# Router products and co-attention weights moved into the normalization of a twelve-layer decoder kernel

## The chip, the cores and the metric

One core of one Trainium2 chip runs the whole program. The metric is the device time of one launch in microseconds (us), as the median of several executions. TensorE is called PE below, VectorE DVE, ScalarE ACT, GpSimd POOL, and SyncE (which issues all DMAs here) SP.

## The reference, cut to what matters

A decoder with four levels works on `x` of 4 batches x 512 tokens x 128 features. Each of its twelve sublayers computes `x = x + f(layernorm(x))`. Three of them are mixtures of experts (stages `l0m`, `l1m`, `l3m` of the kernel, with 16, 64 and 32 experts), and one is a co-attention with a context of 77 tokens per batch (`l1c`). What the change touches of them:

```python
# every expert sublayer, h = layernorm(x)
scores = sigmoid(h @ router_w.T)              # (tokens, experts)
# top groups and top experts of scores + bias; weights w from the chosen scores
out = sum over chosen experts of w * (silu(h @ gate) * (h @ up)) @ down  + shared expert(h)

# co-attention, h = layernorm(x), c = context
similarity = h . w1 + c . w2 + (h * w3) . c + b   # (tokens, 77), softmax over both sides follows
out = [parts made of c, h and the two softmaxes] @ W_qv + b_qv
x = x + out
```

## The kernel before

The program is a row of stages. Each stage is a function that opens blocks (`nc.Block()`); in a block every engine has its own instruction list, and no engine goes on to the next block before all engines have finished this one. Semaphores order the work inside a block. Nothing is scheduled by a planner: each engine runs what the function lists for it, in that order.

Every stage begins with `layernorm` (line 100), one block: DVE and ACT normalize 16 token tiles of `T.X` into `T.LNX` (L142, L171), PE transposes them batch by batch into four PSUM banks (L162), and the banks are copied into `T.LNT`, batches 0 and 2 by ACT (L176) and batches 1 and 3 by DVE (L149). `T.LNT` holds features on partitions and tokens along the row.

`expert_ffn` (line 882) is the expert stage. In the block behind the normalization PE first makes the router products of all 16 tiles (L1079), then the shared expert (`shared_up`, L1028 and L1029, and `shared_down`, L1035). A float32 product of 512 columns shows as two matmul instructions. Meanwhile ACT rounds `T.LNT` into `x_hi` (L1155) and the first expert weights into `w_hi` (L1121), and POOL makes the remainders `x_lo` (L1207) and `w_lo` (L1203). When the router products are there, ACT takes the sigmoid (L1160, `score`), and DVE selects the groups and experts (`route`: L1305, L1280 to L1291, L863 to L868, L1316 to L1335, L1356), with products of the shared expert (L1236) put between its steps. The combine weights are then transposed (L1100), copied, stored and fetched again by SP, and the expert loop begins. PE may run two shared products ahead of DVE (`AHEAD = 2`). In stage `l3m` the weights come as bfloat16 and ACT first widens router and shared weights (L1150, L1153).

`l1_coattention` (line 1582) makes two small arrays first on DVE: `c3`, the context times w3 plus w1 (L1719), and `w2` (L1720). PE then makes the product L1685, after it the similarities of a batch (L1624), and DVE and ACT the softmax over the context (`centre`, `exponentials`, `normalize`: L1732 to L1743). POOL adds the bias to all of `T.X` (L1793), which `close(0)` waits for. Names in the trace drop trailing digits, so `l1c_c` is `c3` and `l1c_w` is `w2`, `w14` or the weights.

## Time and profile before

| | |
|---|---|
| median of 3 runs | 2343.5 us (2336.73 to 2348.67) |
| the profiled execution, its own time | 2343.47 us |
| its span in the trace | 2341.7 us |
| busy: PE, DVE, ACT, POOL | 2088.5, 1676.8, 1215.5, 1153.7 us |
| where the four stages begin (their normalization's first DMA) | l0m 322.4, l1c 484.7, l1m 546.5, l3m 2190.6 us |

The time is what the host's clock on the device gives for a launch; the span is from the first to the last recorded instruction. Busy time of an engine says nothing about which engine is waited for at a given place; that has to be read at that place.

### The profile page before, as it was taken

How to read it: one execution, taken by the hardware profiler on the slowest of the kernel's cores; microseconds unless marked ns; L12 is line 12 of the kernel's file. 1: busy time of each engine (PE TensorE's matmuls, PEld its weight loads, DVE VectorE, ACT ScalarE, POOL GpSimd, SP SyncE). 2: the span in 40 equal slices, each digit the busy share in tenths (PEclk: the TensorE clock that was granted, in tenths of full speed). 3: DMA queues.
4: the chain of work that ended last, by engine and by line, in shares of the span. 5: the costliest groups of instructions: out<-in, count | busy, mean ns of one | idle time of the engine just before them, and what ended most of it. 6: DMA issues, size and time to landing. Idle time of an engine off the chain costs nothing. (4 is left out here: it accounts for less than half of the span.)

```text
span 2341.7 us, 37726 instructions
## 1 busy us (share of the span) xinstructions
PE 2088.5 (89%) x12788; PEld 1458.2 (62%) x12788; DVE 1676.8 (72%) x3556; ACT 1215.5 (52%) x2598; POOL 1153.7 (49%) x1344
## 2 busy tenths in 40 slices
PE   6999779768999987759999999999999986879888
PEld 3666557555788865536666666666666644547666
DVE  5777767756788875557777777777766664469578
ACT  6888645523566653625445444544444443444455
POOL 5333026201699960148776666667666613004255
PEclk8999979968999999979999999999999998989899
DMA  1000007000776620023333433333343331000085
GB/s 51 3 3 3 8 18 160 8 6 22 170 156 155 156 68 1 14 72 60 90 95 84 106 72 100 87 98 95 84 92 72 80 92 42 1 1 1 14 205 124
DMA packets 65048, 161.92 MB, mean 69 GB/s; under 512 B 8139, under 2 KB 19147, under 8 KB 57560
## 3 DMA queue, kind: packets, MB, share of 16 engines
q1 hardware_dynamic: 64856, 159.50, 29.1%
q8 instruction: 103, 1.69, 0.3%
q14 instruction: 89, 0.73, 0.1%
HBM read 156.46 MB, written 3.01 MB: 68 GB/s over the span
## 5 line engine op out<-in xcount | busy, mean ns | idle before, releaser
L2821 ACT ACTIVATE l2h_prT<-bank 128x512 f32<-128x512 f32 x256 | 151.8, 593 | 261.9 <-PE bank L2708 261.9
L2719 PE MATMUL bank<-l2h_og,l2h_wo 128*128 128x512 f32 x512 | 260.3, 592 | 1.6 <-DVE LNT L2980 1.6
L2829 ACT ACTIVATE l2h_pr<-twin,l2h_nmx 128x512 f32<-128x512 f32 x256 | 175.8, 687 | 155.7 <-PE bank L2708 127.8
L1215 POOL TENSOR_TENSOR l1m_hid_lo<-l1m_hid,l1m_hid_hi 128x512 fp32r<-128x512 f32 x128 | 209.8, 1658 | 45.8 <-ACT l1m_hid_hi L1142 45.3
L2956 DVE TENSOR_TENSOR l2h_vg<-bank,l2h_gv 128x512 f32<-128x512 f32 x256 | 175.4, 685 | 76.6 <-PE bank L2682 62.1
L3058 POOL TENSOR_TENSOR l2h_vs<-l2h_vg 128x256 f32<-128x256 f32 x256 | 188.7, 737 | 32.0 <-DVE l2h_vg L2956 31.8
L2983 DVE TENSOR_REDUCE l2h_nmx<-twin 128x2 f32<-128x1024 f32 x128 | 156.1, 1220 | 46.9 <-PE twin L2697 46.8
L3053 POOL TENSOR_TENSOR l2h_plain<-l2h_plain,l2h_rotated 128x512 f32<-128x512 f32 x64 | 82.1, 1283 | 211.2 <-DVE l2h_rotated L2949 211.2
L2968 DVE TENSOR_TENSOR l2h_og<-bank,l2h_gt 128x512 f32<-128x512 f32 x256 | 173.2, 679 | 2.2 <-PE bank L2719 1.6
L2708 PE MATMUL bank<-ident,l2h_pr 128*128 128x128 f32 x1024 | 161.4, 280 | 0.6 <-ACT l2h_prT L2821 0.6
L2708 PEld LDWEIGHTS bank<-ident,l2h_pr 128*128 128x128 f32 x1024 | 117.3, 141 | 69.4 <-issue 46.4
L2682 PE MATMUL bank<-l2h_w_hi,l2h_x_hi 128*128 128x512 f32 x256 | 149.8, 585 | 4.4 <-DVE l2h_vg L2956 4.3
L405 ACT ACTIVATE l0a_pr<-l0a_sc,l0a_nmx 128x128 f32<-128x128 f32 (+3 forms) x256 | 133.3, 553 | 22.1 <-DVE l0a_nmx L290 21.2
L1265 DVE TENSOR_TENSOR l1m_hid<-l1m_prod,l1m_c 128x512 f32<-128x512 f32 x128 | 136.5, 1066 | 4.4
L3061 POOL TENSOR_TENSOR l2h_vs<-l2h_vs 128x128 f32<-128x128 f32 x256 | 122.4, 478 | 20.1
L2733 PE MATMUL bank<-l2h_prT,l2h_v 128*64 128x256 f32 x1024 | 124.6, 385 | 0.0
L1177 ACT ACTIVATE l1m_gate<-bank 128x512 f32<-128x512 f32 x128 | 76.6, 599 | 85.5 <-PE bank L1020 85.5
L2439 POOL TENSOR_TENSOR l3x_pr<-l3x_pr,l3x_rs 128x1232 f32<-128x1232 f32 x16 | 36.0, 2250 | 171.6 <-DVE l3x_rs L2461 171.6
L1257 DVE TENSOR_TENSOR l1m_prod<-bank,l1m_gate 128x512 f32<-128x512 f32 x128 | 88.1, 688 | 44.0 <-ACT l1m_gate L1177 34.5
L2719 PEld LDWEIGHTS bank<-l2h_og,l2h_wo 128*128 128x128 f32 x512 | 95.6, 189 | 27.7 <-issue 4.2
L479 PE MATMUL bank<-ident,l0a_pr 128*128 128x128 f32 x640 | 100.3, 286 | 12.4 <-ACT l0a_prT L397 6.9
L1015 PE MATMUL bank<-l1m_x_hi,l1m_w_hi 128*128 128x512 f32 x256 | 101.1, 395 | 3.9 <-DVE l1m_prod L1257 3.9
(627 smaller groups left out, 5758.1 us busy)
## 6 DMA issues: line engine op xcount, KB each, us to landing
l2h_gt<-l2m_gate_rows SPq DMA_DIRECT2D x128, 512.0 KB, 6.8
l1m_c<-l1m_weights SPq DMA_DIRECT2D x62, 512.0 KB, 6.4
l3m_c<-l3m_weights SPq DMA_DIRECT2D x30, 512.0 KB, 6.7
l0m_c<-l0m_weights SPq DMA_DIRECT2D x14, 512.0 KB, 6.9
l1m_w<-in_l1m_pairs SPq DMA_DIRECT2D x32, 192.0 KB, 6.4
l2h_fresh<-in_l2m_wqkv SPq DMA_DIRECT2D x8, 768.0 KB, 4.1
l2h_wo<-in_l2m_wo SPq DMA_DIRECT2D x8, 512.0 KB, 3.8
l0m_w<-in_l0m_pairs SPq DMA_DIRECT2D x8, 192.0 KB, 5.3
```

The costliest lines, as they stand in the source:

```text
L405: nc.scalar.activation(pr[:, k % RING, r, 0:W], sc[:, k % RING, r, 0:W], ACT.Exp, bias=nmx[:, k % RING, r:r + 1], scale=-1.0).then_inc(exp ...
L1215: nc.gpsimd.tensor_tensor(hid_lo[:, h % RING, :], hid[:, h % HELD, :], hid_hi[:, h % RING, :], ALU.subtract)\
L1265: nc.vector.tensor_tensor(hid[:, h % HELD, :], p, cslot[s][:, blk * S:(blk + 1) * S], ALU.mult).then_inc(hidden, 1)
L2682: out = nc.tensor.matmul(pj[at % 2][:, :], x[:, b * S + t * P:b * S + (t + 1) * P], w[:, QK + h * S:QK + (h + 1) * S], start=(p == 0), sto ...
L2708: out = nc.tensor.transpose(tbank[:, c * P:(c + 1) * P], pr[:, h, c * P:(c + 1) * P], T.ident[:, :])
L2719: nc.tensor.matmul(ybank[:, :], wo[s][:, e, :], og[:, e % 4, :], start=(e == 0), stop=(e == E - 1))\
L2821: nc.scalar.activation(prT[:, j // 2 % 2, h, :, j % 2 * P:(j % 2 + 1) * P], tbank[:, :].rearrange("p (c q) -> p c q", c=TPB), ACT.Copy).th ...
L2829: nc.scalar.activation(pr[:, h, :], sbank[:, h, :], ACT.Exp, bias=nmx[:, k % 2, h:h + 1], accum_out=rs[:, g % 2, t, h:h + 1]).then_inc(exp ...
L2956: nc.vector.tensor_tensor(vg[:, u % 2, :, :], pj[at % 2][:, :].rearrange("p (e d) -> p e d", e=E), spread(gv_h[s][:, b * TPB + t, h, :], H ...
L2968: nc.vector.tensor_tensor(og[:, e % 4, :], obank[g % 2][:, :], gt[:, e // 4, e % 4, :], ALU.mult)\
L2983: nc.vector.tensor_reduce(nmx[:, k % 2, :], sbank[:, :, :], axis=AX, op=ALU.max, negate=True)\
L3058: nc.gpsimd.tensor_tensor(vs[:, u % 2, :, :], vg[:, u % 2, 0:4, :], vg[:, u % 2, 4:8, :], ALU.add)\
```

## The change

Three things are done.

1. `layernorm` gets a hook `route`: after its transposes PE waits for the copy of batch c into `T.LNT` and calls `route(pe, c)`. The expert stages use it for their router products, so these are in the normalization's block. In `l3m` the widening of router and shared weights is done by ACT at the end of the same block (`aside`).
2. In the next block of the expert stages ACT begins with the sigmoid. `w_hi` of the first slot comes behind it (in `l0m` and `l1m`), and the four `x_hi` copies come behind `shared_gate(0)` and `shared_gate(1)`. POOL's list is the same, and its `x_lo` waits for `x_hi`.
3. In `l1_coattention` ACT makes `w2` and `c3` at the end of the normalization's block. The addition of the bias to `T.X` is moved from POOL to DVE, between `bring_rows(0)` and `normalize(1)`.

```diff
@@ layernorm, PE @@
                 last.then_inc(T.ln_turned, 1)
+            for c in range(B if route is not None else 0):
+                pe.wait_ge((T.ln_even_copied, T.ln_odd_copied)[c % 2], B // 2 * n + c // 2 + 1)
+                route(pe, c)
@@ expert_ffn @@
-        layernorm(nc, T, T.X[:, :, :], T.LNX[:, :, :], T.LNT[:, :], loads, loaded, begun=begun)
+        def routed_products(pe, c):
+            if c == 0:
+                if half_weights:
+                    pe.wait_ge(widened, 1)
+                else:
+                    pe.wait_ge(loaded, 16 * len(loads))
+            for t in range(c * TPB, (c + 1) * TPB):
+                bank, at = divmod(t, per_bank)
+                last = nc.tensor.matmul(T.bank[bank][:, at * E:(at + 1) * E], T.LNT[:, t * P:(t + 1) * P],
+                                        wide_router[:, :], start=True, stop=True)
+            if c == B - 1:
+                last.then_inc(logits, 1)
+        def widen_router(act):
+            if half_weights:
+                act.wait_ge(loaded, 16 * len(loads))
+                nc.scalar.activation(wide_router[:, :], router[:, :], ACT.Copy).then_inc(widened, 1)
+                nc.scalar.activation(shared[:, :, :], shared_raw[:, :, :], ACT.Copy).then_inc(widened, 1)
+        layernorm(nc, T, T.X[:, :, :], T.LNX[:, :, :], T.LNT[:, :], loads, loaded, begun=begun, route=routed_products,
+                  aside=(nothing, nothing, widen_router))
...
@@ expert_ffn, ACT @@
-                for c in range(B):
-                    nc.scalar.activation(x_hi[:, c * S:(c + 1) * S], T.LNT[:, c * S:(c + 1) * S], ACT.Copy).then_inc(x_high, 1)
-                if not half_weights:
-                    split_weights(0, 0)
                 act.wait_ge(logits, 1)
...
                 last.then_inc(scored, 1)
+                if not half_weights:
+                    split_weights(0, 0)
                 for g in range(PRE):
                     shared_gate(g)
+                    if g < 2:
+                        round_rows(2 * g)
+                        round_rows(2 * g + 1)
@@ l1_coattention @@
+            act.wait_ge(loaded, 16 * len(loads))
+            nc.scalar.activation(w2[:, :], T.zeros[:, :], ACT.Identity, bias=cols[:, 1:2])
+            nc.scalar.activation(c3[:, :], T.CTXT[:, :], ACT.Identity, bias=cols[:, 0:1], scale=cols[:, 2:3])
...
-                nc.vector.tensor_scalar(c3[:, :], T.CTXT[:, :], cols[:, 2:3], cols[:, 0:1], ALU.mult, ALU.add)
-                nc.vector.tensor_scalar(w2[:, :], T.zeros[:, :], cols[:, 1:2], None, ALU.add).then_inc(prepared, 1)
...
+                    if b == 0:
+                        link(nc.vector.tensor_tensor(T.X[:, :, :], T.X[:, :, :], tiled(bias[:, :], NT), ALU.add))
...
-            @block.gpsimd
-            def _(pool):
-                pool.wait_ge(loaded, 16 * len(loads))
-                nc.gpsimd.tensor_tensor(T.X[:, :, :], T.X[:, :, :], tiled(bias[:, :], NT), ALU.add).then_inc(biased, 1)
```

ACT's list in stage `l0m`, from its last copy of the normalization to its second gate. `L106` and `L1116` (after: `L1139`) are the ends of blocks, ACT_TABLE_LOAD loads the function table for the activation behind it. Before:

```order
L176 ACTIVATE LNT<-twin 128x512 [waits ln_turned]
L106 UNCONDITIONAL_BRANCH
L1116 UNCONDITIONAL_BRANCH [waits barrier_Pool_Activation_PE_DVE_SP_release]
L1155 ACTIVATE l0m_x_hi<-LNT 128x512 [waits l0m_loaded]
L1155 ACTIVATE l0m_x_hi<-LNT 128x512 x3
L1121 ACTIVATE l0m_w_hi<-l0m_w 128x384 [waits l0m_arrived0]
L1160 ACT_TABLE_LOAD
L1160 ACTIVATE l0m_score<-bank 128x256 [waits l0m_logits]
L1128 ACT_TABLE_LOAD
L1128 ACTIVATE l0m_gate<-bank 128x512 [waits l0m_up_done] x2
```

After:

```order
L179 ACTIVATE LNT<-twin 128x512 [waits ln_turned]
L106 UNCONDITIONAL_BRANCH
L1139 UNCONDITIONAL_BRANCH [waits barrier_Pool_Activation_PE_DVE_SP_release]
L1177 ACT_TABLE_LOAD [waits l0m_logits]
L1177 ACTIVATE l0m_score<-bank 128x256 [waits l0m_loaded]
L1144 ACTIVATE l0m_w_hi<-l0m_w 128x384 [waits l0m_arrived0]
L1151 ACT_TABLE_LOAD
L1151 ACTIVATE l0m_gate<-bank 128x512 [waits l0m_up_done]
L1173 ACTIVATE l0m_x_hi<-LNT 128x512 x2
L1151 ACTIVATE l0m_gate<-bank 128x512 [waits l0m_up_done]
L1173 ACTIVATE l0m_x_hi<-LNT 128x512 x2
L1144 ACTIVATE l0m_w_hi<-l0m_w 128x384 [waits l0m_arrived1]
```

The table load for the sigmoid stood behind five activations and now is the first thing in its block, and `x_hi` has moved behind the gates.

PE's list in the same stage, from its last transposes to the shared expert. Before:

```order
L162 MATMUL twin<-ident,LNX 128x128 x3
L106 UNCONDITIONAL_BRANCH
L1010 UNCONDITIONAL_BRANCH [waits barrier_Pool_Activation_PE_DVE_SP_release]
L1079 MATMUL bank<-l0m_router,LNT 128x16 [waits l0m_loaded]
L1079 MATMUL bank<-l0m_router,LNT 128x16 x15
L1028 MATMUL bank<-LNT,l0m_shared 128x512
```

After:

```order
L162 MATMUL twin<-ident,LNX 128x128 x3
L957 MATMUL bank<-l0m_router,LNT 128x16 [waits l0m_loaded,ln_even_copied]
L957 MATMUL bank<-l0m_router,LNT 128x16 x3
L957 MATMUL bank<-l0m_router,LNT 128x16 [waits ln_odd_copied]
L957 MATMUL bank<-l0m_router,LNT 128x16 x3
L957 MATMUL bank<-l0m_router,LNT 128x16 [waits ln_even_copied]
L957 MATMUL bank<-l0m_router,LNT 128x16 x3
L957 MATMUL bank<-l0m_router,LNT 128x16 [waits ln_odd_copied]
L957 MATMUL bank<-l0m_router,LNT 128x16 x3
L106 UNCONDITIONAL_BRANCH
L1038 UNCONDITIONAL_BRANCH [waits barrier_Pool_Activation_PE_DVE_SP_release]
L1056 MATMUL bank<-LNT,l0m_shared 128x512 [waits l0m_loaded]
```

The 16 router products stood behind the end of the block and now stand before it.

DVE's list in `l1c` where the first batch ends: `l1c_hq` and `l1c_ehq` are the last steps of `bring_rows(0)`, `l1c_rs` the first of `normalize(1)`. After (before, the same rows without L1811):

```order
L1787 COPY l1c_hq<-twin 128x512 [waits l1c_hq_done]
L1788 TENSOR_TENSOR l1c_ehq<-twin,LNT 128x512
L1811 TENSOR_TENSOR X<-X,l1c_bias 128x2048
L1770 TENSOR_REDUCE l1c_rs<-l1c_sim 128x4 [waits l1c_expd,dve_step]
L1771 RECIPROCAL l1c_rs<-l1c_rs 128x4 [waits dve_step]
```

The addition to `X` came to DVE, ahead of the second batch's normalization.

## Rows read from the trace of the kernel before

**Rows 1.** Timeline around the start of l1c's block: start us, us, engine, line [idle before]

```profile
489.53 0.60 ACT L176 ACTIVATE LNT<-twin 128x512 f32<-128x512 f32 x1 [0.18 <-PE twin L162]
490.39 0.69 DVE L149 COPY LNT<-twin 128x512 f32<-128x512 f32 x1 [1.02 <-PE twin L162]
...
491.37 4.49 POOL L1793 TENSOR_TENSOR X<-X,l1c_bias 128x2048 f32<-128x2048 f32 x1 [62.41 <-POOLq L106]
491.67 4.37 DVE L1719 TENSOR_SCALAR l1c_c<-CTXT,l1c_cols 128x308 f32<-128x308 f32 x1 [0.58 <-DVEq L106]
...
496.29 1.39 PE L1685 MATMUL bank<-CTXT,l1c_w 128*128 128x308 f32 x2 [5.93 <-DVE l1c_w L1720]
```

**Rows 2.** DVE's groups, 323 to 620 us, then the page's for l1m: count | busy us, mean ns

```profile
L1552 DVE TENSOR_TENSOR X<-X,l1a_bo 128x2048 f32<-128x2048 f32 x1 | 2.3, 2280 | 0.0
...
L1318 DVE TENSOR_TENSOR l0m_outT<-l0m_outT 128x256 f32<-128x256 f32 x1 | 0.4, 424 | 0.0
...
L1281 DVE TENSOR_TENSOR l0m_outT<-l0m_outT 128x128 f32<-128x128 f32 x1 | 0.3, 277 | 0.0
...
L1265 DVE TENSOR_TENSOR l1m_hid<-l1m_prod,l1m_c 128x512 f32<-128x512 f32 x128 | 136.5, 1066 | 4.4
```

**Rows 3.** Timeline of l1c, end of the second batch's normalization

```profile
510.13 0.48 DVE L1743 TENSOR_TENSOR l1c_sim<-l1c_sim,l1c_rs 128x308 f32<-128x308 f32 x1
...
511.17 1.06 PE L1634 MATMUL twin<-ident,l1c_sim 128*77 128x128 f32 x4
```

**Rows 4.** Timeline of l1m's beginning

```profile
552.18 0.69 DVE L149 COPY LNT<-twin 128x512 f32<-128x512 f32 x1 [1.01 <-PE twin L162]
...
553.17 7.06 PE L1079 MATMUL bank<-l1m_router,LNT 128*128 128x64 f32 x32 [1.03 <-PEq L106]
...
555.77 1.28 ACT L1160 ACT_TABLE_LOAD   x1
...
560.27 1.08 ACT L1160 ACTIVATE l1m_score<-bank 128x512 f32<-128x512 f32 x2 [3.22 <-PE bank L1079]
...
561.47 1.23 DVE L1305 TENSOR_TENSOR l1m_outT<-l1m_score,l1m_bias 128x1024 f32<-128x1024 f32 x1 [8.60 <-ACT l1m_score L1160]
561.84 1.92 PE L1029 MATMUL bank<-LNT,l1m_shared 128*128 128x512 f32 x2
...
563.79 0.60 ACT L1128 ACTIVATE l1m_gate<-bank 128x512 f32<-128x512 f32 x1 [1.13 <-PE bank L1029]
...
566.71 0.29 DVE L1291 TENSOR_TENSOR l1m_c<-l1m_c 128x128 f32<-128x128 f32 x1
```

**Rows 5.** Timeline of l0m's beginning

```profile
329.06 4.54 PE L1079 MATMUL bank<-l0m_router,LNT 128*128 128x16 f32 x32 [1.03 <-PEq L106]
329.75 4.95 POOL L1207 TENSOR_TENSOR l0m_x_lo<-LNT,l0m_x_hi 128x512 fp32r<-128x512 f32 x4 [11.44 <-ACT l0m_x_hi L1155]
...
333.64 0.38 ACT L1160 ACTIVATE l0m_score<-bank 128x256 f32<-128x256 f32 x1 [0.70 <-PE bank L1079]
...
334.13 0.84 DVE L1305 TENSOR_TENSOR l0m_outT<-l0m_score,l0m_bias 128x256 f32<-128x256 f32 x1 [5.37 <-ACT l0m_score L1160]
...
334.65 1.17 POOL L1203 TENSOR_TENSOR l0m_w_lo<-l0m_w,l0m_w_hi 128x384 fp32r<-128x384 f32 x1
335.01 0.97 DVE L1280 TENSOR_TENSOR l0m_outT<-l0m_outT 128x128 f32<-128x128 f32 x1
```

**Rows 6.** Timeline of l3m's beginning

```profile
2198.02 6.26 PE L1079 MATMUL bank<-l3m_wide_router,LNT 128*128 128x32 f32 x32 [2.10 <-ACT l3m_wide_shared L1153]
...
2204.32 0.60 ACT L1160 ACTIVATE l3m_score<-bank 128x512 f32<-128x512 f32 x1 [3.07 <-PE bank L1079]
...
2219.63 0.69 DVE L1402 SCALAR_TENSOR_TENSOR l3m_cw<-bank,l3m_cw 128x512 f32<-128x512 f32 x1 [1.72 <-PE bank L1093]
```

**Rows 7.** Windows: length, PE, PEld, DVE, ACT, POOL busy us (instructions), granted clock, DMA share, GB/s

```profile
330.00:332.00 2.00, 2.00 (x19) 2.00 (x18) 0.00 (x0) 1.98 (x5) 2.00 (x2) 0.94 0.00 0
...
2196.00:2198.00 2.00, 0.00 (x0) 0.01 (x1) 0.64 (x1) 1.12 (x5) 0.00 (x0) 1.00 0.00 0
```

More of the change, by code:

```diff
@@ L97, in roots_next, with layernorm @@
     nc.scalar.activation(T.rooted[:, :], T.zeros[:, 0:1], ACT.Sqrt)
[L100 removed]
+def layernorm(nc, T, src, dst, dstT, loads=(), load_sem=None, more=(), more_sem=None, begun=(), times=None, aside=None, route=None, columns=None, eps=1e-5, zeros=()):
     n = T.ln_calls
@@ L175, in _ @@
                 if columns is None:
-                    nc.scalar.activation(dstT[:, c * S:(c + 1) * S], T.bank[c][:, :], ACT.Copy)
+                    nc.scalar.activation(dstT[:, c * S:(c + 1) * S], T.bank[c][:, :], ACT.Copy).then_inc(T.ln_even_copied, 1)
                 else:
                     nc.scalar.activation(dstT[:, c * S:(c + 1) * S], T.bank[c][:, :], ACT.Identity, bias=columns[:, 1:2],
-                                         scale=columns[:, 0:1])
+                                         scale=columns[:, 0:1]).then_inc(T.ln_even_copied, 1)
             if aside is not None:
@@ L1075, in _ @@
                 if half_weights:
-                    pe.wait_ge(widened, 1)
-                for t in range(NT):
-                    bank, at = divmod(t, per_bank)
-                    last = nc.tensor.matmul(T.bank[bank][:, at * E:(at + 1) * E], T.LNT[:, t * P:(t + 1) * P],
-                                            wide_router[:, :], start=True, stop=True)
-                last.then_inc(logits, 1)
+                    pe.wait_ge(widened, 2)
                 for g in range(PRE):
@@ L1147, in take, with round_rows @@
                     nc.scalar.activation(outT[:, c * S:(c + 1) * S], acc[c][:, :], ACT.Copy).then_inc(taken, 1)
+                def round_rows(c):
+                    nc.scalar.activation(x_hi[:, c * S:(c + 1) * S], T.LNT[:, c * S:(c + 1) * S], ACT.Copy).then_inc(x_high, 1)
                 act.wait_ge(loaded, 16 * len(loads))
-                if half_weights:
-                    nc.scalar.activation(wide_router[:, :], router[:, :], ACT.Copy)
-                    if counted:
-                        nc.scalar.activation(tri_round[:, :], tri[:, :], ACT.Copy)
-                    nc.scalar.activation(shared[:, :, :], shared_raw[:, :, :], ACT.Copy).then_inc(widened, 1)
-                for c in range(B):
-                    nc.scalar.activation(x_hi[:, c * S:(c + 1) * S], T.LNT[:, c * S:(c + 1) * S], ACT.Copy).then_inc(x_high, 1)
-                if not half_weights:
-                    split_weights(0, 0)
                 act.wait_ge(logits, 1)
@@ L1163, in _ @@
                 last.then_inc(scored, 1)
+                if counted:
+                    nc.scalar.activation(tri_round[:, :], tri[:, :], ACT.Copy)
+                if not half_weights:
+                    split_weights(0, 0)
                 for g in range(PRE):
                     shared_gate(g)
+                    if g < 2:
+                        round_rows(2 * g)
+                        round_rows(2 * g + 1)
                     if 1 <= g < SLOTS - 1 and not half_weights:
@@ L3237, in build @@
         T.bank = single[0:2] + [T.twin[:, 0, :], T.twin[:, 1, :]] + single[2:6]
-        T.dve_step, T.ln_var, T.ln_std, T.ln_scaled, T.ln_even, T.ln_odd, T.ln_turned, inputs, stored = (
+        T.dve_step, T.ln_var, T.ln_std, T.ln_scaled, T.ln_even, T.ln_odd, T.ln_turned, T.ln_even_copied, T.ln_odd_copied, inputs, stored = (
             ctx.enter_context(nc.semaphore(n))
-            for n in ("dve_step", "ln_var", "ln_std", "ln_scaled", "ln_even", "ln_odd", "ln_turned", "inputs", "stored"))
+            for n in ("dve_step", "ln_var", "ln_std", "ln_scaled", "ln_even", "ln_odd", "ln_turned", "ln_even_copied", "ln_odd_copied", "inputs", "stored"))
         with nc.Block() as block:
```

25 lines of the change are left out of this document (12 added, 13 removed).

## The prediction, made before the changed kernel was run

> **What bounds the kernel at the places that change.** The page of the profile has PE busy for most of the span, but the four places are short stretches in which PE mostly waits, so I read the timeline of each from its last copy into `LNT` on, then DVE's groups by shape for the length of one operation alone, then windows for the granted clock.
>
> In the expert stages the chain is: transposes, the copies, the end of the block, the router products (L1079), the sigmoid, and then DVE's selection. In `l1m` PE ends its transposes at 553.17 - 1.03 = 552.14 and stands idle until the last copy (ending 552.18 + 0.69 = 552.87) and the end of the block (another 0.30) let it begin; the products end at 560.23, and DVE sat idle for 8.60 us until the scores were there [rows 4]. ACT did not lose time on the sigmoid's table: the load ran at 555.77, and ACT then waited 3.22 us more for PE [rows 4]. `l0m` has the same picture, with 1.03 us of PE idle and 4.54 us of products [rows 5], and in `l3m` PE waited 2.10 us, since ACT had to widen the weights first [rows 6]. From the scores on DVE has hardly a gap, so in `l0m` and `l1m` what delays DVE delays the stage. In `l3m` PE's shared products and counts end last: DVE waited 1.72 us for L1093 [rows 6]; but that row of products starts from DVE's first shared product, so it too moves with the scores.
>
> In `l1c` the reader should look at L1719: 128x308 in 4.37 us, starting 0.3 us after POOL's 4.49 us addition and ending 0.18 us after it (491.37 + 4.49 = 495.86 against 496.04), while PE waits 5.93 us for the array behind it [rows 1]. An operation of that size takes well under 0.5 us (128x256 with two inputs: 0.424) [rows 2]. DVE was shut out for the length of POOL's instruction.
>
> **l1c, start.** ACT's two activations come behind its copy that ends at 490.13, and DVE's copy holds the block open to 491.08 [rows 1]. One activation of 128x512 takes 0.60, so two smaller ones take under 1.0 and end at about 491.1: hidden, or at most 0.1 late. PE can begin L1685 at 491.08 + 0.30 = 491.4 instead of 496.29: **-4.9**. If the cover were gone, all of their 1.0 us would show.
>
> **l1c, the addition on DVE.** The same operation of the stage before took 2.28 us on DVE [rows 2]. It stands ahead of `normalize(1)`, which ended at 510.61, and PE took it up at 511.17 [rows 3], so 0.56 is covered: **+1.7**. Queued behind it on DVE is the whole second batch, for which PE waits. With nothing else to do PE would be late by 2.3 (upper end). Sum for l1c **-3.2**, bounds -4.9 and -2.5.
>
> **Router products.** PE loses no time at the block's end any more, but ACT now waits for all products, the end of the block (0.30) and, since the table load is the first thing behind it, 1.28 us that were hidden. l1m: 552.14 + 7.06 + 0.30 + 1.28 = 560.78 against 560.27 [rows 4]: **+0.5**. l0m: 328.03 + 4.54 + 1.58 = 334.15 against 333.64 [rows 5], +0.5; but there the clock was at 0.94 between 330 and 332, nearly its upper level, and 19 products went in 2.00 us [rows 7]; if all 32 go at that pace (3.4) the sum is -0.6. I take **0.0**. l3m: ACT's widening of the router is done some 0.4 after PE's last transpose (2198.02 - 2.10 = 2195.92), an estimate from a tile far smaller than the 0.60 one; 2196.3 + 6.26 + 1.58 = 2204.15 against 2204.32 [rows 6], -0.2; but the clock stood at 1.00 from 2196 to 2198 while PE idled [rows 7], a time that the products now use; at the pace of rows 7 for the first 2.5 us, which does some 23 of 32, it is -2.2. I take **-1.1**. Were l0m's at the lower clock throughout, it would be at +2.1 (32 x 0.19, nearly the pace of l3m).
>
> **What x_lo now meets.** Before, POOL's four `x_lo` (4.95 us, 1.27 each) ran while DVE was idle, all but the end [rows 5]. That end is instructive. L1305, 128x256, took 0.84 against 0.424 for L1318 of the same shape, and L1280, 128x128, 0.97 against 0.277 for L1281 [rows 2, 5]; each ended just behind a POOL instruction (334.70, 335.82). One DVE operation passed between two POOL instructions, no more. So a two-input operation of SBUF operands pays 1.27 in place of its own step for each `x_lo` that is running, about 1.0 in place of it for each `w_lo` (L1280's end minus L1305's: 1.01). Now `x_hi` follows the gates: in l1m the gate can run at about 563.7 (score end 561.9, `w_hi` 0.5, the second table load 1.28), and `x_lo` begins near 564.9. DVE's ten steps from the end of L1305 (562.70) to L1291 (566.71) take 0.40 on average [rows 4], and eight or nine are still ahead at 564.9. Four `x_lo` and two `w_lo` fall on them: 4 x (1.27 - 0.35) + 2 x (1.01 - 0.35) = **+5.0** for l1m. l0m: the collision of rows 5 (0.42 + 0.69 = 1.1) is gone, since POOL is idle when L1305 and L1280 run; the selection of groups (L863 to L868, steps of 0.25) meets the four `x_lo` and two `w_lo` instead, 4 x 1.0 + 2 x 0.75 = 5.5, of which I take five sixths as one will meet a PSUM operation: 4.6 - 1.1 = **+3.5**. l3m: behind L1393 DVE runs one-input searches, and only L1395 and L1356 meet `x_lo`; PE is the later one there [rows 6], so **0**, at most +2.
>
> The other price for such a meeting is a share, not a lock: in l1m's loop L1265 averages 1.066 us, with POOL at work beside it, against 0.69 for a 128x512 step alone [rows 2, 4], 0.38 for each; but those meet only in part, and rows 5 are nearer to a queue on both sides. By 0.38 for each of 12 meetings the two stages would be at +4.6 - 1.1 in place of +8.5.
>
> The Trainium skill (SBUF — State Buffer, Who interferes with whom) says that a DVE instruction with two SBUF inputs and a GpSimd one that reads SBUF exclude each other for a whole instruction, and that issue order decides who blocks. By that rule the 5.0 and 4.6 hold and this part of the change costs time; the trace agrees in L1719 and L1280 above, and nothing in it shows whether a long queue of POOL's could pass DVE twice. With one `x_lo` more passing each time the price would grow by another 2 to 3 us per stage.
>
> **Sum.** -3.2 (l1c) + 0.0 + 3.5 (l0m) + 0.5 + 5.0 (l1m) - 1.1 (l3m) = +4.7. The profiled execution took 2343.47, 1.8 more than its span and equal to the median of the runs, so 2348.2. What a measurement of this kernel can tell from no change is about 0.5%, 11.7 us; the runs shown spread over 12.
>
> **Rivals.**
> (a) DVE gets past POOL cheaply: the loop's price. -3.2 + 0.0 + 0.5 - 1.1 - 1.1 + 4.6 = -0.3: 2343. With no meetings at all, -4.9: 2338.6. For it speaks that POOL's instructions may start at other moments than I placed them; against it rows 5. Chance 0.24.
> (b) Faster by more than 0.5%: the clock. PE is active without the 1.03 us gap, and the stages start earlier, so the rise to the upper level can fall at another place. At the pace of rows 7, l1m's products take 3.4 at least in place of 7.06 (-3.7); l1c lasts from 484.7 to 546.5, and if PE goes at the upper level for 8 us more of it, that gives 4, an estimate. Together with no meetings that is -4.9 - 3.7 - 4 = -12.6: 2331. It decides only if the rise comes early in at least two of the three stages. Chance 0.06.
> (c) PE goes cold in l1m. Its third shared product waits for DVE's first, which comes behind the meetings, so PE idles some 8 us there instead of 2 to 3, the clock falls to its lower level of 1.2 GHz, and each shared product takes 1.92 [rows 4] and not the half of it. With three products for each of the groups that are left, two or three groups at the lower level cost 2.9 each: +6 to +9 more, 2354 to 2357. Chance 0.18, half of it beyond 0.5%.
> (d) The move does nothing in the expert stages, since table load and block end eat what the gap gave, and the meetings are met by waits that were there anyway: only l1c is left, 2340. Chance 0.10; it lies in my range.
> The forecast itself: 0.42, with a range of its own of 2344 to 2352 from the bounds above.
>
> **Numbers.** Faster by over 0.5%: 0.06. Slower: 0.12, from (c) and a double price of the lock. Within: 0.82. The range takes in (a), (d) and most of (c): 2337 to 2355.
>
> **What would show it.** Right: L1685 starts 0.3 us after the copy of batch 3 in l1c; the addition on DVE at 2.3 us, with PE idle 1.7 before the second batch's transposes; in l0m and l1m a table load of 1.28 between the last router product and the score; two-input steps of DVE in the selection at 1.0 to 1.3 us each beside POOL's `x_lo`. Wrong: such steps at their own 0.25 to 0.43; a score more than 1 us earlier in l1m; another granted clock in the routers. The prediction fails as a whole if the loops behind, over 2000 us, change by more than the sum through another phase of clock or DMA, of which no row tells.

## The result, and the profile of the changed kernel

The changed kernel took 2356.2 us in the median of its 22 runs, the kernel before 2346.9 in the median of its 22 beside them: ratio 1.0035, 95% interval 1.0019 to 1.0051. By the ratio it is slower by 8.2 us, with 4.5 to 12.0 as the interval: 0.35%, clear of no change and below the 0.5% that the prediction took as its limit. The prediction had +4.7 us and a range of 2337 to 2355. In absolute time the median lies 1.2 us above the range's end; but the kernel before came out 3.4 us above the median that the prediction was made against, and the ratio put on that median (2343.5) gives 2351.7, inside the range.

The sum in the prediction is made of stretches at the start of four stages, so the trace of the changed kernel (span 2358.7 us, 17 above that of before, where the medians differ by 9) is read at those stretches. It is one execution; the experiments below say which of its readings others repeat. Its timeline in `l1c`, one row per group of instructions (start us, us, engine, line, output<-input, idle before):

```profile
498.24 0.69 DVE L149 COPY LNT<-twin 128x512 f32<-128x512 f32 x1 [0.76 <-PE twin L162]
498.42 0.63 ACT L1646 ACTIVATE l1c_c<-CTXT,l1c_cols 128x308 f32<-128x308 f32 x1
...
499.35 0.76 PE L1717 MATMUL bank<-CTXT,l1c_w 128*128 128x308 f32 x2 [1.15 <-PEq L106]
...
510.86 2.27 DVE L1811 TENSOR_TENSOR X<-X,l1c_bias 128x2048 f32<-128x2048 f32 x1
...
514.42 1.13 PE L1667 MATMUL twin<-ident,l1c_sim 128*77 128x128 f32 x4 [2.27 <-DVE l1c_sim L1772]
```

L1717 starts 0.42 us after the last copy's end (498.93), where its counterpart L1685 started 5.21 after it [rows 1]: -4.8. ACT's second new activation ends at 499.05, so the two cost 0.1 at most. The addition takes 2.27 on DVE, and PE waits all of it in front of the second batch. The whole stage, from its normalization's first DMA to that of the next stage, went from 61.8 to 55.1 us: -6.7, where these two items give -2.5. The rest, 4.2, I put down to the clock. The first 10 us of the stage, as windows (columns as in [rows 7]), of the changed kernel and then of the kernel before:

```profile
492.78:502.78 10.00, 5.89 (x34) 5.38 (x34) 6.10 (x17) 6.76 (x15) 0.00 (x0) 0.75 0.13 34
```

```profile
484.68:494.68 10.00, 3.65 (x16) 3.22 (x16) 7.14 (x14) 5.77 (x12) 3.31 (x1) 0.50 0.12 34
```

0.75 against 0.50: in this execution PE reached its upper level within the first 10 us.

`l0m`, from the router products on:

```profile
330.04 3.89 PE L957 MATMUL bank<-l0m_router,LNT 128*128 128x16 f32 x32
...
334.27 1.28 ACT L1177 ACT_TABLE_LOAD   x1 [4.25 <-PEq L106]
...
336.52 0.29 DVE L1304 TENSOR_TENSOR l0m_outT<-l0m_outT 128x128 f32<-128x128 f32 x1
...
338.87 0.22 DVE L869 TENSOR_REDUCE l0m_outT<-l0m_outT 128x16 f32<-128x64 f32 x1
338.99 4.94 POOL L1231 TENSOR_TENSOR l0m_x_lo<-LNT,l0m_x_hi 128x512 fp32r<-128x512 f32 x4 [18.47 <-ACT l0m_x_hi L1173]
339.13 1.21 DVE L870 TENSOR_TENSOR l0m_outT<-l0m_outT 128x64 f32<-128x64 f32 x1
...
340.37 1.20 DVE L871 SCALAR_TENSOR_TENSOR l0m_outT<-l0m_outT 128x64 f32<-128x64 f32 x1
...
342.21 0.21 DVE L866 TENSOR_REDUCE l0m_outT<-l0m_outT 128x16 f32<-128x64 f32 x1
...
342.83 1.19 DVE L868 TENSOR_TENSOR l0m_outT<-l0m_outT,rev 128x64 f32<-128x64 f32 x1
```

The table load stands in the open between the last router product and the score. The old collision (0.97 us for a 128x128 step [rows 5]) is gone, 0.29 now: that gives 1.1 back, with L1305's part. In its place three small steps (the first, L871 behind it and L868) take 1.2 each as soon as POOL's `x_lo` run, while a reduction with one input passes beside them in its own 0.21. The fourth `x_lo` falls beside a shared product of DVE that reads PSUM. The `w_lo` behind them cost 0.4, 0.7 and 0.6 more (L870 at 344.30 in 0.66, L871 at 345.00 in 0.92, L1340 at 346.56 in 0.86). The selection (from DVE's addition of the bias to its end) grew from 15.6 to 19.3 us and began 0.3 sooner: +3.4.

`l1m`:

```profile
560.61 1.28 ACT L1177 ACT_TABLE_LOAD   x1 [7.29 <-PEq L106]
...
565.68 0.42 DVE L1310 TENSOR_TENSOR l1m_c<-l1m_c 128x256 f32<-128x256 f32 x1
565.90 5.61 POOL L1231 TENSOR_TENSOR l1m_x_lo<-LNT,l1m_x_hi 128x512 fp32r<-128x512 f32 x4 [132.69 <-ACT l1m_x_hi L1173]
566.03 1.50 DVE L1311 TENSOR_TENSOR l1m_c<-l1m_c 128x256 f32<-128x256 f32 x1
...
567.46 1.50 DVE L1312 TENSOR_TENSOR l1m_c<-l1m_c 128x256 f32<-128x256 f32 x1
...
569.00 1.37 DVE L1313 TENSOR_TENSOR l1m_c<-l1m_c 128x256 f32<-128x256 f32 x1
570.40 1.26 DVE L1310 TENSOR_TENSOR l1m_c<-l1m_c 128x128 f32<-128x128 f32 x1
571.45 2.07 POOL L1227 TENSOR_TENSOR l1m_w_lo<-l1m_w,l1m_w_hi 128x384 fp32r<-128x384 f32 x2
571.59 1.08 DVE L1311 TENSOR_TENSOR l1m_c<-l1m_c 128x128 f32<-128x128 f32 x1
572.58 1.08 DVE L1312 TENSOR_TENSOR l1m_c<-l1m_c 128x128 f32<-128x128 f32 x1
573.70 0.29 DVE L1313 TENSOR_TENSOR l1m_c<-l1m_c 128x128 f32<-128x128 f32 x1
...
575.18 2.04 PE L1063 MATMUL bank<-l1m_hid,l1m_shared 128*128 128x512 f32 x2 [8.20 <-DVE l1m_hid L1260]
577.02 1.91 PE L1056 MATMUL bank<-LNT,l1m_shared 128*128 128x512 f32 x2
...
580.99 0.69 DVE L1260 TENSOR_TENSOR l1m_hid<-bank,l1m_gate 128x512 f32<-128x512 f32 x1 [1.77 <-ACT l1m_gate L1151]
...
581.60 0.86 DVE L1340 TENSOR_SCALAR l1m_c<-l1m_c 128x128 f32<-128x128 f32 x1
...
582.66 1.02 PE L1063 MATMUL twin<-l1m_hid,l1m_shared 128*128 128x512 f32 x2
```

Six POOL instructions (four `x_lo`, two `w_lo`), and six DVE steps, one to each. They take 7.79 us together; by themselves they are three of 0.42 and three of 0.28 [rows 2], 2.1: +5.7. So is the stretch that holds them, from DVE's addition of the bias to its first shared product: 11.25 where it was 5.56. When POOL is done, the next step is back at 0.29. Behind them PE has idled 8.20 us, and its next products take 1.9 to 2.0 a pair, and from 580.09 on 1.02 again. The windows of that stretch (columns as in [rows 7]) have the granted clock beside it:

```profile
562.00:569.00 7.00, 4.98 (x7) 1.64 (x5) 5.80 (x7) 6.29 (x11) 3.10 (x3) 0.71 0.00 0
569.00:575.00 6.00, 0.00 (x0) 0.00 (x0) 5.86 (x8) 0.06 (x1) 4.51 (x4) 0.54 0.00 0
```

PE does nothing from 569 to 575, and the clock stands at 0.54 of full, about its lower level of 1.2 GHz; after it the pairs take what they take at that level. That is rival (c), by its own sign. The two rows of DVE show what it costs. Its second shared product begins 5.81 us behind PE's first output product, after 1.77 us of waiting for PE and ACT; in the kernel before it began 4.06 behind it (571.93 - 567.87) without a wait:

```profile
571.93 0.69 DVE L1236 TENSOR_TENSOR l1m_hid<-bank,l1m_gate 128x512 f32<-128x512 f32 x1
...
572.54 0.35 DVE L1316 TENSOR_SCALAR l1m_c<-l1m_c 128x128 f32<-128x128 f32 x1
```

That is +1.75. From there to the end it is +0.50 (15.74 us in place of 15.24), one step: the TENSOR_SCALAR behind it now falls on a `w_lo` and takes 0.86 in place of 0.35. The selection ends 48.9 us after the stage's start, where it was 40.7: +8.2, made of +0.2 until DVE begins, +5.7 of meetings, and these 2.3.

`l3m`: the router products now follow the transposes closely, but at the lower level throughout:

```profile
2212.43 7.00 PE L957 MATMUL bank<-l3m_wide_router,LNT 128*128 128x32 f32 x32
```

That is 7.00 us where it was 6.26 [rows 6], and the table load follows, at 2219.78; DVE's first step begins 15.06 us into the stage where it was 14.43, and the selection behind it is as long as before: +0.6.

In this one execution the length of `l1c` and the ends of the three selections sum to -6.7 + 3.4 + 8.2 + 0.6 = +5.5.

### The profile page after: what moved, and what is told of

Same layout as the page of the kernel before. It is cut to its first block and busy times, and to the rows that moved or that the text cites. A ratio compares the mean times of both kernels' runs of the same rounds, so it can differ in the third digit from the quotient of the medians.

```text
span 2358.7 us, 37730 instructions
## 1 busy us (share of the span) xinstructions
PE 2100.2 (89%) x12788; PEld 1460.9 (62%) x12788; DVE 1686.2 (71%) x3555; ACT 1215.0 (52%) x2600; POOL 1151.3 (49%) x1343
## 5 line engine op out<-in xcount | busy, mean ns | idle before, releaser
L3085 POOL TENSOR_TENSOR l2h_vs<-l2h_vs 128x128 f32<-128x128 f32 x256 | 122.5, 478 | 20.1
```

## The experiments

Each was timed in five rounds beside the kernel before on its chip. "Selection" is the stretch on DVE from the addition of the bias to the end of the weights `cw`; its end is given from the stage's first DMA. Diffs are against the changed kernel where nothing else is said.

**The rows' halves made inside the normalization.** ACT makes `x_hi` and POOL `x_lo` behind each batch's copy, while DVE has nothing to add, so that the meetings go and the rest of the change stays.

```diff
+            for c in (0, 1, 2, 3):
+                act.wait_ge((T.ln_even_copied, T.ln_odd_copied)[c % 2], B // 2 * n + c // 2 + 1)
+                nc.scalar.activation(x_hi[:, c * S:(c + 1) * S], T.LNT[:, c * S:(c + 1) * S], ACT.Copy).then_inc(x_high, 1)
...
+        def remainders(pool):
+            for c in range(B):
+                pool.wait_ge(x_high, c + 1)
+                nc.gpsimd.tensor_tensor(x_lo[:, cols], T.LNT[:, cols], x_hi[:, cols], ALU.subtract).then_inc(x_low, 1)
...
-                    if g < 2:
-                        round_rows(2 * g)
-                        round_rows(2 * g + 1)
```

> The changed kernel, with x_hi and x_lo made in the normalization's block (ACT and POOL beside PE's router products) instead of behind the gates. Theory (two-input steps of DVE's selection are locked out by POOL's x_lo, and in l1m PE goes cold while it waits): the selection in l0m ends 3.5 to 4.6 us earlier after the stage's start than with the change (30.8 us), in l1m some 6 to 8 us earlier (48.9 us), l3m about the same; together 10 to 13 us less than the changed kernel, which puts it at 2343 to 2346, a ratio to the kernel before of 0.998 to 1.000. Rival (the loss is another phase of clock or DMA in the loops and untouched stages): selections may shorten, but the whole stays at the changed kernel's ratio, 1.0035.

Ratio 1.0024 (1.0003 to 1.0046), and not the 0.998 to 1.000 expected. `l0m`'s selection took 15.9 us in place of 19.3 (before: 15.6), but it began 1.7 later: POOL's `x_lo` now hold the normalization's block open, and PE waits 2.13 us for its end. So it ended 1.8 earlier, where 3.5 to 4.6 were expected. In `l1m` the six long steps became two, beside the two `w_lo` that were left:

```profile
560.02 1.70 POOL L1233 TENSOR_TENSOR l1m_w_lo<-l1m_w,l1m_w_hi 128x384 fp32r<-128x384 f32 x1 [3.24 <-ACT l1m_w_hi L1156]
560.91 1.37 DVE L1306 TENSOR_TENSOR l1m_c<-l1m_outT 128x512 f32<-128x512 f32 x1
...
567.49 2.05 PE L1075 MATMUL bank<-l1m_hid,l1m_shared 128*128 128x512 f32 x2 [6.68 <-DVE l1m_hid L1262]
```

From DVE's addition of the bias to its first shared product it took 7.00 us, not 11.25 (before: 5.56): the four `x_lo` are 4.3 of that loss, and the two `w_lo` left are 1.4. (Counted from the stage's start, that product came at 20.9 instead of 26.5, but 1.3 of it is that the selection began earlier, with router products of 4.38 us.) PE still waited 6.68 and went on at the lower level, and `l1m`'s selection still ended 3.0 later than in the kernel before. `l3m`'s ended 1.7 later than in the changed kernel; two kernels that don't touch it show the same. The overall ratio's interval overlaps that of the changed kernel, so the stage's rows carry this, not the ratio.

**The sigmoid's table loaded early**, by an activation of one column of zeros inside the normalization:

```diff
                 nc.scalar.activation(shared[:, :, :], shared_raw[:, :, :], ACT.Copy).then_inc(widened, 1)
+            nc.scalar.activation(T.rooted[:, :], T.zeros[:, 0:1], ACT.Sigmoid)
```

> The changed kernel, with one dummy sigmoid of 128x1 at the end of ACT's list in the normalization of each expert stage, so that the table load runs beside the router products. If the exposed load is on the path, the scores come 1.28 us earlier in each of the three stages, and the whole is 3.8 us less than the changed kernel (ratio to before about 1.002). If the selection only waits for other things, as the meetings with POOL, which then begin at the same place, the gain is under 2 us.

Ratio 1.0018 (1.0000 to 1.0037). The score follows the block's start with no load between:

```profile
557.91 1.08 ACT L1178 ACTIVATE l1m_score<-bank 128x512 f32<-128x512 f32 x2 [3.22 <-PEq L106]
```

DVE began 11.39 us into `l1m` in place of 15.24, 3.9 earlier: 1.3 of it is the load, and 2.6 are the 32 router products, which took 4.36 in this execution and 6.93 in that of the changed kernel. The meetings stayed (1.50, 1.49, 1.37, 1.24, 1.08, 1.08), and the selection ended at 44.7. In `l0m` it began 1.4 earlier but ended only 0.6 earlier (it took 20.1 in place of 19.3), in `l3m` it was 1.3 at both ends. The exposed load is real: it is all that is gained against the four kernels below whose router products are as fast as here (their selection in `l1m` begins at 12.7 to 12.8).

**The two halves of the change apart**: the expert stages alone (with the co-attention function of before), and the co-attention alone (with the expert stages of before). The first one's edit, which the second leaves out:

```diff
-        layernorm(nc, T, T.X[:, :, :], T.LNX[:, :, :], T.LNT[:, :], loads, loaded, aside=(nothing, nothing, similarity_weights))
+        layernorm(nc, T, T.X[:, :, :], T.LNX[:, :, :], T.LNT[:, :], loads, loaded)
...
+                nc.vector.tensor_scalar(c3[:, :], T.CTXT[:, :], cols[:, 2:3], cols[:, 0:1], ALU.mult, ALU.add)
+                nc.vector.tensor_scalar(w2[:, :], T.zeros[:, :], cols[:, 1:2], None, ALU.add).then_inc(prepared, 1)
```

> The changed expert stages with the co-attention of before. Theory: all of the loss is here: l0m +3.4, l1m +8.2, l3m -1 to +1, so +10.5 to +12.5 us and a ratio of 1.0045 to 1.0055. Rival (the co-attention's change shifts the phase of the clock for what follows and so causes part of the loss): under +8, ratio at most 1.0035.

> The kernel before with the changed co-attention alone. Theory by the sum: -3.2 us (4.9 gained at the start, 1.7 lost to the addition on DVE), ratio 0.9986; by the trace of the changed kernel, where the stage is 6.7 shorter, up to -6.7, ratio 0.9971. Rival: a stage that follows gives it back, ratio 1.000.

Experts only: 1.0044 (1.0018 to 1.0069); `l1m`'s selection ends at 46.9, `l0m`'s at 30.7, `l1c` takes 61.9. Co-attention only: 1.0013 (0.9992 to 1.0034), `l1c` 58.6 us long, -3.2. The stage did what the sum said, but the kernel did not: a gain of 3.2 us is a ratio of 0.9986, outside the interval, and the rival's 1.000 lies in it. In this execution `l1m`, which the edit doesn't touch, took 323.4 us in place of 319.8; whether the edit causes that isn't shown. The two ratios sum to 1.0057, which with their intervals agrees with the whole's 1.0035. The loss is in the expert stages. In the co-attention's own execution the granted clock was 0.50 for the first 30 us of `l1c`, and PE's wait behind the addition is another:

```profile
516.01 1.14 PE L1643 MATMUL twin<-ident,l1c_sim 128*77 128x128 f32 x4 [0.84 <-DVE l1c_sim L1748]
```

0.84 in place of 2.27: PE's eight products in front of it were slower and covered more. So the addition costs PE 0.8 at the lower clock and 2.3 at the upper.

**PE kept busy, too short.** Eight products whose result nobody reads, between PE's last gate product and its wait for DVE in `l1m`, with all else as changed:

```diff
                     if g == 1:
                         pe.wait_ge(scored, 1)
+                        for _ in range(8 if NSH == 2 else 0):
+                            nc.tensor.matmul(acc[3][:, :], shared[:, 0, 0:P], T.LNT[:, 0:S], start=True, stop=True)
```

> The changed kernel, and in l1m PE makes eight extra products of 512 columns into a bank that is free, behind the second shared product, where it stood idle for 8.2 us. It separates two parts of l1m's loss. If the selection is late by the lock alone, nothing moves: hid0 (DVE's first shared product) to the end of the selection stays 22.4 us. If part of it is PE gone cold, that stretch falls to 20.1 as in the kernel before, and the stage to about 325 us (from 327.9), 2 us less. The products of the extra work add nothing to the output.

Ratio 1.0028 (1.0004 to 1.0052), and no gain at the place: from DVE's first shared product to the selection's end 22.7 us (changed kernel 22.4, before 20.1). The timeline of PE says why:

```profile
562.09 7.03 PE L1110 MATMUL twin<-LNT,l1m_shared 128*128 128x512 f32 x16
573.13 2.08 PE L1063 MATMUL bank<-l1m_hid,l1m_shared 128*128 128x512 f32 x2 [4.01 <-DVE l1m_hid L1262]
```

They ended 4.0 us before the wait did. The same with the halves in the normalization and four products gave no gain either, where 20.1 to 21 were expected (it stood at 22.7 there too, though PE was idle for only 3.16 us):

> The kernel with x_hi and x_lo in the normalization, with four such extra products in l1m. There PE stood idle for 6.7 us and then ran at the lower clock, and the stretch from DVE's first shared product to the end of the selection took 22.8 us. With PE kept busy: 20.1 to 21, the stage some 2 us shorter than in that kernel, the ratio to before about 1.001 (from 1.0024). If the clock falls all the same, 22.8 again.

Ratio 1.0011 (0.9990 to 1.0032).

**PE kept busy, long enough**: the same line with 18 in place of 8.

> The changed kernel with 18 products instead of 8 whose results nobody reads, on TensorE between the shared branch's last gate product and its first output product, in the stages with two shared experts. With 8 they ended at 569.1 us of the profiled execution, 4.0 us before the output product at 573.1, and the granted clock was 1.00 up to 569 and 0.50 from 573 to 579. Theory (the clock fell in the 4 us gap left, and that is most of the 2.2 us that the co-attention experts' selection loses behind its first shared product): 10 more products fill another 4.3 us, the pair of output products takes the upper level's 1.02 us each, and the time from the first shared product to the end of the selection falls from 22.7 to 20.8 to 21.3 us; the kernel is 1.5 us faster than with 8, too little to be seen in a ratio, 1.0022 expected. Rival (the clock falls whatever is there, or the loss is VectorE beside GpSimd's remainders of the weights): that time stays at 22 us or more.

```profile
564.61 15.61 PE L1110 MATMUL twin<-LNT,l1m_shared 128*128 128x512 f32 x36
580.06 1.02 PE L1063 MATMUL bank<-l1m_hid,l1m_shared 128*128 128x512 f32 x2
...
583.53 0.69 DVE L1262 TENSOR_TENSOR l1m_hid<-bank,l1m_gate 128x512 f32<-128x512 f32 x1 [3.79 <-ACT l1m_gate L1153]
...
584.14 0.86 DVE L1342 TENSOR_SCALAR l1m_c<-l1m_c 128x128 f32<-128x128 f32 x1
...
598.06 1.22 DVE L1377 TENSOR_TENSOR l1m_cw<-l1m_cw,l1m_c 128x1024 f32<-128x1024 f32 x1
```

```profile
569.00:573.00 4.00, 4.00 (x11) 1.80 (x10) 3.93 (x4) 0.00 (x0) 4.00 (x5) 1.00 0.00 0
573.00:579.00 6.00, 6.00 (x15) 2.66 (x14) 5.78 (x46) 0.00 (x0) 1.03 (x2) 1.00 0.01 1
```

I had mis-sized the products: one is two records of 0.43 us (16 records for 8, 36 for 18), so 18 last 15.6 us and not 7.8, and the output product came 4.5 us after its input was ready (DVE's at 574.87, plus 0.7). The expected 20.8 to 21.3 was therefore missed: 24.4, and the kernel is no faster (1.0039, 1.0018 to 1.0059). What can be compared is the stretch behind PE's first output product, in two parts: to the start of DVE's second shared product, and from there to the end of the selection.

| kernel | PE idle before it, us | first part | second part | whole stretch, us |
|---|---|---|---|---|
| before | 2.29 | 4.06 | 15.24 | 587.17 - 567.87 = 19.3 |
| changed | 8.20 | 5.81 | 15.74 | 596.73 - 575.18 = 21.6 |
| 8 extra products | 4.01 | 6.23 | 15.74 | 595.10 - 573.13 = 22.0 |
| halves in the normalization | 6.68 | 6.20 | 15.75 | 589.44 - 567.49 = 21.9 |
| the same and 4 extra products | 3.16 | 6.22 | 15.75 | 591.69 - 569.72 = 22.0 |
| 18 extra products | none | 3.47 | 15.75 | 599.28 - 580.06 = 19.2 |

With 18 the granted clock stayed at 1.00. DVE had done all that it could ahead of its second shared product and waited 3.79 us for it, as it waited about 2 us in the three rows above; there PE and ACT needed 6.2 us for it, here 3.47. That is the clock. In the kernel before DVE itself was the later one (4.06, no wait), so the lower clock costs the changed kernel 5.81 - 4.06 = 1.75 us. The other 0.50 is the step beside a `w_lo`, 0.86 in place of 0.35. It is there in this run as well, and the whole stretch is back at 19.2 only because 3.47 is as much below 4.06. The two go together: in the ten traces in which DVE waited for that gate the step took 0.85 or 0.86, in the four in which it didn't 0.34 or 0.35. PE's delay thus costs 2.3 in all, 1.75 directly.

**The addition of `l1c` back on POOL**, in the block's start, so that DVE's queue is free of it:

```diff
-                    if b == 0:
-                        link(nc.vector.tensor_tensor(T.X[:, :, :], T.X[:, :, :], tiled(bias[:, :], NT), ALU.add))
+            @block.gpsimd
+            def _(pool):
+                pool.wait_ge(loaded, 16 * len(loads))
+                nc.gpsimd.tensor_tensor(T.X[:, :, :], T.X[:, :, :], tiled(bias[:, :], NT), ALU.add).then_inc(biased, 1)
```

> The changed kernel with the addition of the co-attention's bias back on POOL; c3 and w2 stay on ACT. The addition (4.5 us) then meets DVE's first two-input step behind the similarities (2.8 us after the block's start), which should end just behind it: 1.5 to 2 us late for the first batch; 2.3 us of DVE are gone from the second. By the lock the stage is 0 to 0.8 us shorter than with the addition on DVE; if the two engines shared, 1.7 us shorter. Ratio to before 1.003 to 1.0035.

```profile
499.86 4.50 POOL L1822 TENSOR_TENSOR X<-X,l1c_bias 128x2048 f32<-128x2048 f32 x1 [66.73 <-POOLq L106]
...
502.97 0.48 DVE L1761 TENSOR_TENSOR l1c_sim<-bank,l1c_drow 128x308 f32<-128x308 f32 x1 [1.15 <-PE bank L1657]
503.48 0.47 DVE L1763 TENSOR_REDUCE l1c_mx<-l1c_sim 128x4 f32<-128x308 f32 x1
503.99 0.71 DVE L1764 TENSOR_TENSOR l1c_sim<-l1c_sim,l1c_mx 128x308 f32<-128x308 f32 x1
...
514.47 1.14 PE L1667 MATMUL twin<-ident,l1c_sim 128*77 128x128 f32 x4 [0.21 <-DVE l1c_sim L1772]
```

PE's wait is down to 0.21, and POOL's 4.50 us cost DVE 0.23: only L1764 (two inputs in SBUF) ran into them and ended 0.3 after POOL, while L1761 (one input in PSUM) and the reduction passed. Expected were 1.5 to 2 us late for the first batch; it was 0.23. With the weights out of the block the addition does hardly any harm where it stood before. `l1c` took 54.8. The ratio, 1.0004 (0.9980 to 1.0028), is lower than the changed kernel's, and than the 1.003 to 1.0035 expected, by more than the 2 us that the addition accounts for; the intervals overlap, and I make nothing of the difference.

**All of it combined**: halves in the normalization, with the first slot's `w_hi` and `w_lo`, the table loaded early, the addition on POOL.

```diff
+            if not half_weights:
+                act.wait_ge(arrived[0], 16)
+                nc.scalar.activation(w_hi[0][:, :], wslot[0][:, :], ACT.Copy).then_inc(w_high[0], 1)
+            nc.scalar.activation(T.rooted[:, :], T.zeros[:, 0:1], ACT.Sigmoid)
...
+            if not half_weights:
+                pool.wait_ge(w_high[0], 1)
+                nc.gpsimd.tensor_tensor(w_lo[0][:, :], wslot[0][:, :], w_hi[0][:, :], ALU.subtract).then_inc(w_low[0], 1)
```

> x_hi, x_lo and the first slot's w_hi and w_lo in the normalization's block, the sigmoid's table loaded there, router products there, the addition of the co-attention's bias on POOL. Lock and table load gone from the selection: against the kernel before the scores come 2 to 3.5 us earlier in l0m and l1m and the selection takes as long as before or 1 us less; the sum -3 (l0m), -4 (l1m), -2 (l3m), -5 (l1c): 14 us less, ratio 0.994. If PE's clock decides instead (it is idle longer before DVE's first shared product), l1m keeps 2 to 3 of it and the ratio is 0.996 to 0.998.

Ratio 0.9973 (0.9957 to 0.9989), 2339.9 us: faster than both kernels, by 6.3 us against before, where 14 were expected. (It lies in the 0.996 to 0.998 of the expectation's other case, but not for its reason: the clock stayed up.) In `l1m`:

```profile
557.00 1.03 POOL L990 TENSOR_TENSOR l1m_w_lo<-l1m_w,l1m_w_hi 128x384 fp32r<-128x384 f32 x1
558.38 2.05 PE L1075 MATMUL bank<-LNT,l1m_shared 128*128 128x512 f32 x2 [3.35 <-PEq L106]
...
564.87 0.97 DVE L1322 TENSOR_TENSOR l1m_c<-l1m_c 128x128 f32<-128x128 f32 x1
...
566.71 1.10 PE L1082 MATMUL bank<-l1m_hid,l1m_shared 128*128 128x512 f32 x2 [3.14 <-DVE l1m_hid L1267]
```

One meeting is left (0.97), PE idles 3.14, its pairs stay at 1.02 and the stretch behind is 586.01 - 566.71 = 19.3 (4.06 and 15.24, as before). The selection ends at 40.0. The price is the first row: POOL's work holds the normalization's block open, and PE waits 3.35 us for its end, so most of what the early router products gain is paid out again.

**Two parts of it, and a control.** The combined kernel with the addition on DVE; the combined expert stages with the co-attention of before; and the kernel before against itself.

> The combined kernel (the rows' high and low halves and the first slot's weights made inside the normalization, the table loaded early), with the co-attention as in the change: its bias addition on VectorE. Theory (the place of the addition is worth 1.7 us of TensorE's wait at most, and costs or gives nothing else): 2343 us, ratio 0.998, the co-attention 55 to 57 us long. Rival (the addition on VectorE costs several us, as the changed kernel's ratio of 1.0035 against 1.0004 with it on GpSimd would have it): ratio 1.000 or above.

> The combined kernel's expert stages with the co-attention of the kernel before. Theory (expert stages and co-attention add up; the latter's part is 3 to 5 us): 2344 us, ratio 0.9990, the co-attention 58 to 62 us and the co-attention experts' selection ending 40 us after the start of their normalization, as in the kernel before (40.7). Rival (the combined kernel's 0.9973 was all the co-attention): ratio 1.000 or above.

> The kernel before, unchanged, timed against itself. Expected ratio 1.0000 within 0.002, and stages of the same lengths as in its first profiled execution except for those that differ between executions (the first sequence attention, the co-attention, the two wide expert stages), by up to 4 us each. A ratio that is off by 0.003 or more would say that what the intervals of the other comparisons claim is too narrow.

0.9973 (0.9956 to 0.9989) with the addition on DVE; 0.9991 (0.9972 to 1.0011) without the co-attention's part; the control 1.0000 (0.9979 to 1.0020). So the place of the addition makes no difference that can be told in the whole; in the stage it does, 58.6 us with it on DVE (55 to 57 expected) and 56.9 with it on POOL. The co-attention's change may give some 4 us here (0.9991 to 0.9973, as its 3.2 us in the stage would have it), but these two intervals overlap. The combined expert stages alone are at no change. In the two partial kernels `l1m`'s selection ended at 41.0 and 41.2 (before 40.7), not at the 40 expected: there PE's pairs behind its wait took 1.5 and 1.9, after only 2.26 us of idling; it had made pairs of 1.9 before the wait too. The control shows how much single traces wander: `l0m`'s selection began at 14.2 us in place of 11.8 and took 14.7 in place of 15.6: the router products took 6.98 us at the lower clock, where they had taken 4.54, and so DVE's first steps missed POOL. It ended 1.5 later, in the same kernel.

## Why the prediction was right, and which sizes were off

**Direction and mechanism held.** Expected was a small loss, and from DVE's meetings with POOL's remainders; +8.2 measured against +4.7. By its own terms:

| term | predicted, us | trace of the changed kernel, us | other traces of the same stage code |
|---|---|---|---|
| `l1c`, start | -4.9 | -4.8 | |
| `l1c`, addition on DVE | +1.7 | +2.3 | 0.8 at the lower clock |
| `l1c`, whole stage | -3.2 | -6.7 | -3.0 to -3.2 in seven kernels |
| `l0m`, score | 0.0 | -0.3 | -0.3 to -0.4 in four |
| `l0m`, meetings | +3.5 | +3.7 | +3.6 or +3.7 in four |
| `l1m`, score | +0.5 | +0.2 | -2.2 or -2.3 in four |
| `l1m`, meetings | +5.0 | +5.7 | +5.7 in four |
| `l1m`, PE's delay behind them | not in the sum | +2.3 | +2.6 in three (all but 18 products) |
| `l3m` | -1.1 | +0.6 | -1.6 or -1.7 in two, +2.3 in two |

The four are the expert stages alone, 8 and 18 extra products, and the addition back on POOL. With what these show (`l1c` -3.2, `l0m` +3.3, `l1m` +6.1, `l3m` -1.7 to +2.3) the sum is +4.5 to +8.5; the changed kernel's own trace gives +5.5; both are inside the measured 4.5 to 12.0. Against the second trace of the kernel before, `l0m` is 1.5 less.

**The lock was read rightly.** The step that one DVE operation passes between two POOL instructions, drawn from two rows [rows 5], held in six out of six in `l1m`. The rule of the Trainium skill (SBUF — State Buffer, Who interferes with whom) that such pairs exclude each other for whole instructions, and that operations with at most one SBUF input don't take part unless they run in one of VectorE's 2-port modes, which it says `tensor_scalar` can enter, agrees with the reductions at 0.21, with L1764 against L1761 above, and with the TENSOR_SCALAR at 0.86. The prediction counted L1719 [rows 1] as a case of two SBUF inputs; its row shows a TENSOR_SCALAR with one tensor, so by the page it falls under that exception; the number (4.37 us beside POOL's addition) stands. The rival price, 0.38 a meeting, is out: in `l1m` `x_lo` cost 0.95 to 1.08 each and `w_lo` 0.80, where 0.92 and 0.66 stood in the sum. They were a little dearer, and POOL's four took 5.61 and not 5.00: it waits for DVE too.

**The term that failed is rival (c), left out of the sum.** The mechanism was described there (PE idle for some 8 us, 8.20 measured; products at 1.9) and given 0.18; it happened. Its price of 6 to 9 was too high: the pairs were back at 1.02 from PE's second output product on, before the second group was through, and DVE had 0.6 us of its own work to hide a part. So it cost 1.75, or 2.3 with the step that it put beside a `w_lo`, rather than two or three groups at 2.9. It should have been part of the forecast, since its cause, the meetings, was. With it the sum is +7.0.

**That the forecast for `l1m` came near is partly luck.** Its score had +0.5 from router products of 7.06 us, and in all ten other kernels that make them early they took 3.68 to 4.51. The prediction had named a score more than 1 us earlier and another clock in the routers as signs of being wrong; both came in the four kernels with the same code, and only the changed kernel's own trace had 6.93. The 2.7 us that this is worth cancel about what rival (c) and the dearer meetings add: +5.5 was forecast for the stage, +6.1 is what the others show.

**`l3m` was optimistic.** The claim that the upper level seen while PE idled would be used by the moved products has a contrary row: 7.00 us at 0.50. Eight more of the eleven kernels with early router products had 7.00 or 7.01, and two had 4.71 and 4.81 (the expert stages alone, and 8 extra products in `l1m`, far ahead of it). The clock at that place is not set by the move alone.

**Rival (b) came in part**: in `l1m`'s router products, as said, and in `l1c`, where PE was at the upper level sooner. That was worth about 4 us in the changed kernel's execution (6.7 less 2.5) and was absent in all seven other kernels with the same co-attention code (58.6 to 58.8 us each), so it is a property of that execution. In the two kernels with the addition back on POOL the stage took 54.8 and 56.9, and the clock rose some 15 to 25 us into it and not after 30; whether the place of the addition does that isn't shown. The ratio over 22 runs holds only the mean.

**Rivals (a) and (d) are out**: the meetings cost their full price in both stages. What the experiments add is the cause: in `l1m` taking `x_lo` out of the selection's way removes 4.3 of the 5.7 us ahead of DVE's first shared product, with the two `w_lo` as the rest, and keeping PE at work until its output product removes the lower clock behind it, though at the price of a later product. At the level of the whole kernel only the three combined kernels are told from the changed one by their ratios; the others rest on the stages' rows. The +8.2 should not be split more finely than this, as stages that no edit touches show: the wide stage `l2m` took 932.9 to 942.0 us over these traces, and `l1a` 49.4 to 53.7.

## What to carry to other kernels

Before moving work forward, ask which idle time the work behind it was using: here GpSimd's remainders ran free while VectorE waited for the scores, and the same six instructions, moved by a few microseconds onto two-input SBUF steps, cost nearly one of GpSimd's own durations each. Then follow the delay one engine further, to a TensorE that idles and resumes at half its clock. A move pays when the helpers move along with it, as in the combined kernel, and what holds a block open is counted.
